# Attention projection of a Macaron block: f32r turns, swapped halves in one product, scaling on ScalarE, and a quarter of the early maxima moved into attention

## The reference

```python
x = x + 0.5 * ffn(layernorm(x))      # mixture of 8 experts, the best 2 of each token
x = x + attention(layernorm(x))      # this change
x = x + 0.5 * ffn(layernorm(x))
```

```python
q, k, v = x @ wq, x @ wk, x @ wv
q, k = q * cos + rotate_half(q) * sin, k * cos + rotate_half(k) * sin
attn = softmax(causal(q @ k.T / sqrt(32)))
out = (attn @ v) @ wo
```

## Time and profile before

| | |
|---|---|
| median of 3 runs | 1275.9 us (1274.03 to 1278.19) |
| the profiled execution | 1275.88 us |
| its span, first to last instruction | 1274.6 us |
| PE, DVE, ACT, POOL busy | 1179.8, 910.2, 659.6, 600.5 us |
| granted TensorE clock, mean | 0.984 of full speed |

### The profile page before, as it was taken

The page is one execution under the profiler, slowest core; times in us unless marked ns, Lnnn a source line. Parts: engine busy times, 40 slices in busy tenths (PEclk is TensorE's granted clock), DMA queues, the critical chain, the costliest instruction groups (busy, mean ns, idle before and its releaser), DMA issues.

```text
span 1274.6 us, 20931 instructions
## 1 busy us (share of the span) xinstructions
PE 1179.8 (93%) x6837; PEld 757.3 (59%) x6837; DVE 910.2 (71%) x2132; ACT 659.6 (52%) x1305; POOL 600.5 (47%) x496
## 2 busy tenths in 40 slices
PE   4899999989998999999999999999999879999996
PEld 3678888758776544444545455445443346777774
DVE  8767777779997776576678787688755675666664
ACT  2545555536455554355456566356567744444442
POOL 4945444313210111001437556556582554888886
PEclk9899999999999999999999999999999999999999
DMA  9923333556530032013445845556633453666665
GB/s 335 367 96 108 111 109 108 174 168 120 96 63 4 34 70 35 1 53 83 99 101 159 173 100 125 174 133 173 135 93 66 139 204 66 100 102 102 101 105 73
DMA packets 68552, 148.44 MB, mean 116 GB/s; under 512 B 8832, under 2 KB 29312, under 8 KB 64448
## 3 DMA queue, kind: packets, MB, share of 16 engines
q0 software_dynamic: 35184, 93.34, 34.4%
q1 hardware_dynamic: 33264, 53.77, 12.4%
HBM read 81.28 MB, written 33.55 MB: 90 GB/s over the span
## 4 chain that ended last, share of the span: by engine, by line
PE 55%; DVE 19%; DMA 9%; issue 8%; POOL 6%; ACT 4%; SPq 0%; DVEq 0%; ACTq 0%; POOLq 0%
PE bank L839 10%; PE bank L1633 8%; PE bank L1645 8%; PE bank L997 7%; PE bank L862 5%; PE bank L1680 5%; DVE PM L1010 4%; PE bank L1663 3%; DVE bank L1012 3%; DMA out<-Y,DI 3%; POOL out L789 3%; DMA CD<-P 2%; DMA XG<-xn,TK 2%; PE bank L821 2%; PE bank L1395 2%
## 5 line engine op out<-in xcount | busy, mean ns | idle before, releaser
L1728 ACT ACTIVATE P<-bank 128x512 f32<-128x512 f32 (+3 forms) x640 | 304.6, 534 | 253.9 <-PE bank L1633 244.4
L1010 DVE TENSOR_REDUCE PM<-bank 128x1 f32<-128x512 f32 x384 | 252.4, 683 | 66.1 <-PE bank L997 65.7
L997 PE MATMUL bank<-Ks,Qs 96*128 96x512 f32 (+3 forms) x640 | 234.9, 387 | 15.1 <-DVE PM L1012 7.8
L1633 PE MATMUL bank<-Qs,Ks 98*128 98x512 f32 (+3 forms) x640 | 241.9, 408 | 5.7 <-ACT P L1728 3.4
L1633 PEld LDWEIGHTS bank<-Qs,Ks 98*128 98x128 f32 x640 | 116.6, 189 | 141.4 <-ACT P L1728 73.5
L1784 POOL TENSOR_SCALAR_AFFINE_SELECT P<-P 128x512 f32<-128x512 f32 x64 | 44.2, 702 | 277.3 <-ACT P L1728 228.8
L997 PEld LDWEIGHTS bank<-Ks,Qs 96*128 96x128 f32 x640 | 121.3, 190 | 64.3 <-DVE PM L1010 22.7
L1645 PE MATMUL bank<-P,V 128*32 128x512 f32 (+3 forms) x1280 | 152.0, 547 | 4.3 <-POOL P L1784 4.3
L1012 DVE CUSTOM_DVE_ANT_0 bank<-bank,KB 128x128 f32<-128x128 f32 (+3 forms) x256 | 124.1, 495 | 40.2 <-PE bank L997 39.6
L789 POOL DMA_INDIRECT out<-Y,DI x78 | 128.1, 1643 | 38.5 <-issue 32.6
L1798 POOL TENSOR_TENSOR CH<-CH,P 128x512 f32<-128x512 f32 x108 | 139.4, 1442 | 14.0 <-ACT P L1728 13.4
(11 more groups left out here) (193 smaller groups left out, 1935.9 us busy)
## 6 DMA issues: line engine op xcount, KB each, us to landing
CD<-P POOLq DMA_DIRECT2D x17, 1024.0 KB, 7.3
xn<-XN SPq DMA_DIRECT2D x8, 1024.0 KB, 7.9
WR<-L_ffn_w POOLq DMA_DIRECT2D x16, 512.0 KB, 15.6
XO<-y POOLq DMA_DIRECT2D x8, 1024.0 KB, 9.4
WR<-L_ffn_w SPq DMA_DIRECT2D x16, 512.0 KB, 7.8
CD<-P SPq DMA_DIRECT2D x7, 1024.0 KB, 5.3
CD<-CH POOLq DMA_DIRECT2D x7, 1024.0 KB, 6.8
XA<-y POOLq DMA_DIRECT2D x24, 256.0 KB, 4.2
```

The source lines that it names most:

```text
L997: pe.matmul(bk(g, bank)[:, 0:n], g.Qs[b][0:96, G % 4 * 4 + h, c * P:c * P + P], g.Ks[0:96, G % 4, k * BQ:k * BQ + n], start=True, stop=Tru ...
L1010: dve.tensor_reduce(dst, bk(g, bank)[:, 0:n], AX.X, ALU.max).then_inc(s(f"free{bank}"), 1)
L1633: pe.matmul(bk(g, bank)[:, o:BQ], g.Ks[0:98, G % 4, k * P:k * P + P], g.Qs[G // 4][0:98, G % 4 * 4 + j, o:BQ], start=True, stop=True).then ...
L1728: act.activation(a.P4[buffer_of(n)][:, j, o:BQ], bk(g, score_bank(g, i))[:, o:BQ], ACT.Exp, scale=scale).then_inc(s("exp"), 1)
```

## The change

- `stack` makes the turns as products with an f32r identity (`p.IR`, copied once by ScalarE) in place of fp32 transposes.
- Only groups 0 to 2 have their maxima in the projection (`EARLY = 3`). From tile 5 on, even tiles take one product after every third from the ninth, odd ones from the twelfth. Group 3 becomes the first in attention's list, and the factor there goes from 1.1 to 1.13. An assertion keeps a buffer of partial maxima from being written before it is read.
- VectorE no longer scales the normed rows: it computes -mean x factor, one column (`shift`), and ScalarE scales with it (`Identity` with scale and bias), behind `doubled`. The small buffer `sm` is doubled.
- The rotation's two half products with the sines become one over all 640 columns, whose input swaps the halves by a reversed step.
- ScalarE's early load of the exponential's table no longer waits for the last scaling.

```diff
+EARLY = 3
-    p.sm = t("smA", [P, 4])
+    p.sm = t("smA", [P, 2, 5])
+    p.IR = t("IR", [P, P], F32R)
...
-    ahead = [key for G in range(4) for key in tops_of(G)]
+    ahead = [key for G in range(EARLY) for key in tops_of(G)]
...
-                if (total - done) % (total // 8) == 0 and done > total // 4 and i > 4 and ahead:
+                if (total - done) % (total // 8) == 0 and done > total // 4 + total // 8 * (i % 2) and i > 4 and ahead:
...
         dve_newton_of_one(g, v, sd, y, u)
-        dve.tensor_scalar(p.X[:, b, :], p.X[:, b, :], p.mv[:, b, 0:1], y, ALU.subtract, ALU.mult).then_inc(s("pxn"), 1)
+        dve.tensor_scalar(shift, p.mv[:, b, 0:1], y, -1.0, ALU.mult, ALU.mult).then_inc(s("shift"), 1)
...
         dve.tensor_tensor(hd(p.t1[:]), qk, p.cs[:, b, 0:32].unsqueeze(1).to_broadcast([P, 20, HD]), ALU.mult)
-        dve.tensor_tensor(hd(p.t2[:])[:, :, 0:16], qk[:, :, 16:32], turn(32), ALU.mult)
-        dve.tensor_tensor(hd(p.t2[:])[:, :, 16:32], qk[:, :, 0:16], turn(48), ALU.mult).then_inc(s("rope"), 1)
+        dve.tensor_tensor(halves_of(p.t2[:]), halves_of(flat[:, 0:640])[:, :, ::-1, :],
+                          p.cs[:, b, 32:64].rearrange("p (a d) -> p a d", a=2).unsqueeze(1).to_broadcast([P, 20, 2, 16]),
+                          ALU.mult).then_inc(s("rope"), 1)
...
+    act.copy(p.IR[:], g.ident)
...
+    def scale(i):
+        act.wait_ge(s("shift"), i + 1)
+        act.activation(p.X[:, i % 4, :], p.X[:, i % 4, :], ACT.Identity, bias=p.sm[:, i % 2, 4:5],
+                       scale=p.sm[:, i % 2, 2:3]).then_inc(s("pxn"), 1)
...
         if i < NT:
             doubled(i)
+        if i + 2 < NT:
+            scale(i + 2)
...
-                ins = pe.transpose(bk(g, bank)[0:96, h * P:h * P + P], Nf[:, 4 * q + h, :], ident)
+                ins = pe.matmul(bk(g, bank)[0:96, h * P:h * P + P], p.N[:, 4 * q + h, :], p.IR[:], start=True, stop=True)
...
-    ahead = [key for G in range(4, 4 * NB) for key in tops_of(G)]
+    ahead = [key for G in range(EARLY, 4 * NB) for key in tops_of(G)]
...
-            while ahead and given < 1.1 * weight:
+            while ahead and given < 1.13 * weight:
                 key = ahead.pop(0)
+                assert key[1] < EARLY + 2 or ("solvemax", key[1] - 2) in plan, key
```

More of the change, by code:

```diff
@@ L1124, in project_plan @@
                 ring.take(("stack", i - 1, q))
-        if told < (64 - len(ahead)) // 16:
+        if told < (16 * EARLY - len(ahead)) // 16:
             g.found[i].append(told)
@@ L1128, in project_plan @@
             told += 1
-    assert told == 4
-    g.shared = [("found", G) for G in range(4)]
+    assert told == EARLY
+    g.shared = [("found", G) for G in range(EARLY)]
 def turned_from_n(g, i):
@@ L1228, in norm @@
         dve.wait_ge(dv.sem, dv.up())
-        dve.tensor_scalar(p.sm[:, 0:1], p.mv[:, b, 1:2], 1e-5, None, ALU.add).then_inc(s("pvar"), 1)
+        dve.tensor_scalar(p.sm[:, i % 2, 0:1], p.mv[:, b, 1:2], 1e-5, None, ALU.add).then_inc(s("pvar"), 1)
     def scale(i):
         b = i % 4
-        v, sd, y, u = (p.sm[:, j:j + 1] for j in range(4))
+        v, sd, y, u, shift = (p.sm[:, i % 2, j:j + 1] for j in range(5))
         dve.wait_ge(s("psd"), i + 1)
         dve_newton_of_one(g, v, sd, y, u)
-        dve.tensor_scalar(p.X[:, b, :], p.X[:, b, :], p.mv[:, b, 0:1], y, ALU.subtract, ALU.mult).then_inc(s("pxn"), 1)
+        dve.tensor_scalar(shift, p.mv[:, b, 0:1], y, -1.0, ALU.mult, ALU.mult).then_inc(s("shift"), 1)
     def low(i):
@@ L1247, in rope_split @@
         qk = hd(flat[:, 0:640])
-        turn = lambda lo: p.cs[:, b, lo:lo + 16].unsqueeze(1).to_broadcast([P, 20, 16])
+        halves_of = lambda ap: ap.rearrange("p (h a d) -> p h a d", a=2, d=16)
         dve.wait_ge(s("pP"), i + 1)
@@ L1306, in root @@
         act.wait_ge(s("pvar"), i + 1)
-        act.activation(p.sm[:, 1:2], p.sm[:, 0:1], ACT.Sqrt).then_inc(s("psd"), 1)
+        act.activation(p.sm[:, i % 2, 1:2], p.sm[:, i % 2, 0:1], ACT.Sqrt).then_inc(s("psd"), 1)
+    def scale(i):
+        act.wait_ge(s("shift"), i + 1)
+        act.activation(p.X[:, i % 4, :], p.X[:, i % 4, :], ACT.Identity, bias=p.sm[:, i % 2, 4:5],
+                       scale=p.sm[:, i % 2, 2:3]).then_inc(s("pxn"), 1)
     def turned(i):
@@ L1339, in act_project @@
     root(0)
+    scale(0)
     turned(0)
     root(1)
+    scale(1)
     for i in range(NT + 1):
@@ L1353, in act_project @@
         if i == NT - 1:
-            act.wait_ge(s("pxn"), NT)
-            act.activation(p.sm[:, 1:2], p.sm[:, 0:1], ACT.Exp)
+            act.activation(p.sm[:, 0, 1:2], p.sm[:, 0, 0:1], ACT.Exp)
 def pe_project(g):
     s, pe, p, ident = g.s, g.nc.tensor, g.p, g.ident
-    Nf = p.N[:].bitcast(F32)
     def transp(i):
@@ L1507, in attend_plan @@
     ring, plan = g.ring, []
-    ahead = [key for G in range(4, 4 * NB) for key in tops_of(G)]
+    ahead = [key for G in range(EARLY, 4 * NB) for key in tops_of(G)]
     later = {}
-    told, weight, given, extra, known, solved, turned, free = 4, 0.0, 0.0, [], [], [], [], True
+    told, weight, given, extra, known, solved, turned, free = EARLY, 0.0, 0.0, [], [], [], [], True
     def put(at, step):
@@ L1741, in scale_last @@
         bank, use = g.ring.where[("proj", 3, c)]
-        act.wait_ge(s("shift"), c + 1)
+        act.wait_ge(s("shift"), NT + c + 1)
         if c == 0:
```

## The result

The changed kernel takes **1282.81 us** (median of 8 runs, 1281.07 to 1286.07), the kernel before 1276.11 on the same chip (8 runs, 1273.06 to 1278.19). The ratio is 1.0048, with a 95% interval of 1.0032 to 1.0064: **slower**, by some 6 us. Forecast were 1272.4 and at most 1278.5, so the prediction was wrong in sign and outside its range. The profiled execution took 1281.07 us (span 1279.8, mean granted clock 0.980 against 0.984).

What follows compares the result with a forecast made beforehand. VectorE was taken to bound projection tiles 5 to 13 and TensorE the other tiles, with little TensorE room in attention. Projection -8.4 and attention +4.9 made -3.5 on 1275.88 us: 1272.4, range 1266.5 to 1278.5.

Steps and rivals of the forecast that it cites:

- the starts of groups 4 and 8: Attention: group 8's maxima transfers, beside GpSimd's 1 MB accumulate, come 1.1 us late, +1.1 (bounds 0 and 5); group 4 in time.
- The third rival: Attention, group 8: its transfers wait out the 1 MB accumulate, 5.7 us late instead of 1.1, total 1277.0; chance 0.07.
- The projection, -8.4: Projection's sum: -6.9 to tile 13, +0.44 for group 2's transposes, -1.8 in tiles 14 and 15, -0.1 in the tail.
- in tiles 5 to 13 that is hidden: Projection: ScalarE's 0.78 us scaling costs nothing there, since ScalarE is busy for 41 of 79 us.
- The turns: no gain: Projection: an f32r turn was taken at 110 ns, as before, so no change; possible range 60 to 190 ns.
- The about -3.6: Projection, six tiles' turns: at 60 ns a turn -6 us, of which ScalarE's bank copies leave about -3.6.
- The fourth rival: Projection: the f32r turns' loads aren't hidden, 190 ns each, total about 1291; chance 0.06.
- The sentence beside the sum: Projection: by the skill's 81 ns, turns shrink until ScalarE's copies hold them, 1.8 us in six tiles, total 1270.6; not summed.
- Attention's price of ten widths: Attention: the moved maxima products, 10 widths of 512, cost 0.33 us each, +3.3, plus 0.5 for transposes and reduction.
- VectorE's price: Attention: moved maxima cost 16 x 0.43 = 6.9 us, plus 0.7; as a rival, total 1276.2, chance 0.18.
- TensorE's slots: Attention: moved maxima cost only TensorE's time, 16 x 0.15 = 2.4 us, plus 0.5; the lower bound of their price.
- the first rival: Attention takes the maxima in TensorE's slots (2.4 and 0.5) and projection turns are cheaper (-1.8): total 1268.6; chance 0.22.

Runs made afterwards that it cites:

- the mended kernel: Changed kernel plus 16 filler products before tile 15's turns and six after, block 1's second residual accumulate later, found maxima copied before ScalarE's scaling: 1271.57 us, ratio 0.9957.
- the run without filler: The mended kernel without its filler products around the last tile's turns: 1276.83 us, ratio 0.9994 to the kernel before.
- the move-only run: The kernel before with only group 3's maxima moved into attention (new places, factor 1.13): 1282.91 us, ratio 1.0063.
- the mended pair of runs: The mended kernel with f32r turns (1271.57 us, ratio 0.9957) and the same with fp32 transposes for the turns (1273.13 us, ratio 0.9953).
- the mended move: The move-only run's kernel plus the later residual accumulate of block 1 and the filler products before the first score: 1275.88 us, ratio 0.9984.
- the mended kernel whose VectorE scales: The mended kernel with the scaling of the normed rows back on VectorE: 1274.88 us, ratio 0.9978 to the kernel before.
- the version with fp32 turns: The changed kernel with the turns again as fp32 transposes by the fp32 identity: 1280.17 us, ratio 1.0036 to the kernel before.

## Why the prediction was wrong

Its last line was wrong through one step and through a term that it did not have; a second step took a part of the gain.

- **The step that failed: "the starts of groups 4 and 8", the +1.1.** The order was foreseen rightly: group 4 in time, group 8's two transfers beside GpSimd's 1 MB, TensorE and ScalarE behind them. The size was not. The 2.85 us of the earlier trace rows, taken for "beside another transfer", stood beside the same kind of 1 MB, but near its end; GpSimd had issued it 6.2 us ahead of the 473.56 (before, GpSimd's timeline):

```profile
467.32 1.30 POOL L1831 DMA_DIRECT2D XO<-y  x1 [4.61 <-DMA XO<-L_attn_x]
```

  At group 8 the 1 MB was issued 2.4 us ahead, and the two transfers stood 4.70 us apart (4.87 to 5.85 in the three other runs with that lead); the wait was 3.98 us and not 1.1. The bound of 5 held the wait, but not what followed it. The third rival, at 0.07, came nearest in mechanism, but the first transfer did not wait the accumulate out: its packets start 3.4 us before the last of the 1 MB end.
- **What was nowhere in it: an idle TensorE can be granted half clock afterwards.** Neither the sum nor a rival has a term for it, though the forecast itself put new idle time ahead of group 8. Group 8 lasted 57.8 us behind the wait and 53.7 in the mended kernel: 4.1 us on top of 3.6 (3.98 less 0.34). At the stage's start it is 2.9 (15.9 against 13.0). Together that is 10.6 us; 2.5 of them the mended kernel spends elsewhere, from group 9 on, with two short stretches of half clock and a wait of 2.80 us for GpSimd's mask, where the changed kernel's is 1.23:

```profile
954.66 1.93 PE L1665 MATMUL bank<-P,V 128*32 128x512 f32 x8 [2.80 <-POOL P L1804]
```

  The page that gives this rule is the Trainium skill's "TensorE: Matmul & The Clock Gate" ("What's actually happening"): the low clock is the default, and activity releases it. The traces agree with the fall, 0.50 behind 3.29 and 3.98 us of idle time and 1.00 where both are gone, but the release came late: from 407.02 to 417.00 TensorE was busy throughout and still at 0.50. It should have been a rival.
- **The clock also falls for short times, in every version.** In attention the kernel before has four stretches of 3.4 us at 0.50 (from 500.6, 548.4, 664.4 and 848.7 us), the changed kernel one (468.2) beside its two long ones. One costs its group some 1.5 us: with group 3's maxima moved, group 9 takes 45.8 us in the six versions that have none in it and 47.3 in the five that have one. Ahead of the one at 548.4 TensorE has no idle time of over 0.8 us, so idle times of this length are not its only cause, and attention's lengths compare to a few microseconds only.
- **The projection, -8.4 against -6.7.** Terms that held: tile 14's products at 5.16 us (384.51 to 389.67; 5.2 was forecast), the joined product at 0.82 (the same as a plain one of 640 columns, so nothing for the reversed step), the ScalarE scaling at 0.82 (0.78 taken). The one that failed is "in tiles 5 to 13 that is hidden": ScalarE had room by its busy share, but its queue has an order, and the maxima's copy stood behind the scaling. With the copy first and nothing else in its way the projection gains 8.0 (132.5, the run without filler). So the sum of -8.4 was near, for a kernel that was not this one. Inside it, the scaling was under-priced (3.7 against 2.3) and the maxima's move over-priced (3.5 in the move-only run, where the sum's terms for it make 4.6).
- **The turns: no gain, as forecast**, for a reason that was half right. At 110 ns a turn nothing was to change; in fact a turn came down to 89 ns, and a set still took 2.28 us, since ScalarE's copies hold it. The about -3.6 that "the bank copies on ScalarE leave", for a turn of 60 ns, has no row behind it. The fourth rival (loads not hidden) is dead: a load lasts longer (170 ns in the mean against 126 of the earlier trace rows) and stays hidden. The Trainium skill ("TensorE: Matmul & The Clock Gate", "Back-to-back issue gap") has about 81 ns for a pair of load and product at N=128, near the 89 here. The sentence beside the sum allowed for the copies and still expected 1.8 us; the mended pair of runs shows none.
- **Attention's price of ten widths: not above the forecast.** +3.3 and +0.5 were forecast, 3.8 in all. Attention grows by 3.1 us in the mended kernel, 3.2 in the mended move and 2.0 in the mended kernel whose VectorE scales (590.7). VectorE's price (6.9 and 0.7) does not fit. TensorE's slots (2.4 and 0.5), the first rival's price, fit as well as the one taken; the short half clocks leave that open.
- **Adding it up.** From the -3.5 of the forecast, with 1.7 less gained in the projection, 2.9 more of wait at group 8, 4.1 of half clock behind it and 2.9 at the stage's start, one comes to +8.1; the profiled executions differ by +5.2. The rest is not taken apart; attention's lower price and the short stretches of half clock, four before and one after, point that way. The forecast's terms without group 8's are -8.4 + 3.8 = -4.6. The mended kernel, which has neither of the two long stretches, gained 5.0 by the medians and 5.5 by the ratio.
- The share of 0.12 for "slower" leaned mostly on the fourth rival, which did not happen; the third was priced without the clock. With 4.1 us of half clock on its 1277.0 it would have been 1281.1, and with the 2.9 at the stage's start 1284.0.

What stays open: why the kernel before kept its clock behind 2.67 us of idle time at attention's start while versions with 2.9 to 3.3 us lost it. Nor is the length of the half clock explained: 13.7 us behind 2.90 us of idle time in one version, 3.4 behind 3.20 in another. No run shortened or lengthened that one wait alone.

## What to carry to other kernels

When a change makes an engine wait, look at what is next in its queue, not at its busy share: a copy of 0.56 us behind a new scaling cost 4 us of a stage (140.5 against 136.3), and swapping two lines gave it back. Small transfers on which a whole group waits should be issued ahead of a large one; moving work between stages shifts them past each other although neither is edited. A new wait of TensorE can cost twice its length (3.6 us of it and 4.1 of half clock here; with the fp32 turns the same wait cost group 8 only 1.0 beyond itself), and where real work can't fill it, products that compute nothing are worth trying.

## What was not expected of the hardware

- Behind 3 to 4 us of idle time TensorE worked at half clock for 3 to 17 us, although it was busy for most of them. The same wait of 3.9 us at group 8 was followed by nearly 14 us of it in the changed kernel, and by 3 to 4 in the version with fp32 turns.
- In two of the runs the clock fell for some 7 us behind only 1.10 us of idle time, ahead of which stood 3.2 us of bf16 filler and a set of turns. With six more products in that place it stayed at 1.00 in all four versions that had them.
- A 16 KB transfer took 1.45 us to the issue of the next when alone, 2.85 when issued 6.2 us behind a 1 MB accumulate and 4.70 to 5.85 when issued 2.4 us behind it.
- A VectorE product of 128x640 whose input swaps 16-element halves by a negative step takes 815 ns, one without it 825.
- An f32r weight load of 96 columns takes 170 ns in the mean, an fp32 one 126, and yet the pairs with the f32r load follow each other faster (89 against 110 ns).
